# A mixture-of-experts stage in units of 128 rows instead of 256, written out with constant waits

## What is computed

```python
xn = layernorm(x)
x = x + gnn(xn, edges, weights) + linear_attention(xn)      # stages 1 and 2
h = layernorm(x)                                            # stage 3
gate_logits = h @ Wg + bg + bias                            # 8 experts
topk_vals, topk_idx = top_k(gate_logits, 2)
topk_w = softmax(topk_vals)
hid = relu(einsum('td,edh->teh', h, W1) + b1)               # 256 -> 512
y = einsum('teh,ehd->ted', hid, W2) + b2                    # 512 -> 256
x = x + sum over the two chosen experts of topk_w * y
```

## Time and profile before

| | us |
|---|---|
| median of 3 runs | 3915.12 |
| lowest and highest of them | 3912.13, 3915.24 |
| the profiled execution | 3911.73 |
| its span in the profile | 3910.0 |
| TensorE busy (share of the span) | 2910.5 (74%) |
| VectorE busy | 2598.6 (66%) |
| GpSimd busy | 2539.5 (65%) |
| mean granted TensorE clock | 0.898 of full speed |
| expert stage, first transposes to the last add's issue | 3056.66 to 3904.03 |

### The profile page before, as it was taken

How to read it: one execution, slowest core, us unless ns; L and a number is a source line. 1 busy time by engine, 2 the same in 40 slices (tenths; PEclk the granted TensorE clock), 3 DMA queues, 4 the chain that set the end, 5 groups by cost and what they waited for, 6 DMA issues and landing times. The chain is left out here.

```text
span 3910.0 us, 52671 instructions
## 1 busy us (share of the span) xinstructions
PE 2910.5 (74%) x16406; PEld 2397.2 (61%) x16407; DVE 2598.6 (66%) x6331; ACT 639.2 (16%) x1335; POOL 2539.5 (65%) x2431
## 2 busy tenths in 40 slices
PE   5957777476666666666776777777765799999998
PEld 5846666255555555555555555555532688888887
DVE  8899888165555555556888888888876444454444
ACT  8212222310000000000000000000023121222221
POOL 0048888577777777777777777777726478744444
PEclk9997777789898989888999898899887899999999
DMA  5857775533443433344444444444373365544443
GB/s 180 269 172 218 214 209 162 185 119 119 118 118 118 119 116 118 118 118 124 130 128 128 131 130 129 125 131 130 116 243 112 81 114 120 119 78 71 73 72 55
DMA packets 348241, 521.28 MB, mean 133 GB/s; under 512 B 54265, under 2 KB 267773, under 8 KB 348029
## 3 DMA queue, kind: packets, MB, share of 16 engines
q0 software_dynamic: 130944, 275.64, 28.0%
q1 hardware_dynamic: 166547, 187.72, 16.0%
q10 hardware_dynamic: 50537, 55.32, 4.5%
HBM read 378.21 MB, written 140.28 MB: 133 GB/s over the span
## 5 line engine op out<-in xcount | busy, mean ns | idle before, releaser
L721 POOL DMA_INDIRECT message<-h_table,records x1660 | 1597.2, 962 | 541.5 <-issue 527.0
L1213 PE MATMUL bank<-message,select 128*128 128x256 f32 x3320 | 894.7, 418 | 389.9 <-issue 344.8
L1780 DVE TENSOR_TENSOR acc<-acc,bank 128x256 f32 x1660 | 698.8, 421 | 552.1 <-PE bank L1213 383.8
L1213 PEld LDWEIGHTS bank<-message,select 128*128 128x128 f32 x3320 | 661.9, 207 | 577.0 <-issue 424.8
L682 POOL DMA_INDIRECT lists<-placed,dest_i x300 | 384.4, 1281 | 324.7 <-ACT placed L898 240.9
L765 POOL DMA_INDIRECT out<-acc,row_of x224 | 350.8, 1566 | 358.9 <-DVE acc L2189 236.5
L1773 DVE TENSOR_SCALAR select<-iota_n,records 128x128 f32<-128x128 f32 x1660 | 466.2, 361 | 14.6 <-ACT acc L939 12.7
L1461 PE MATMUL bank<-w,acc 128*128 x1792 | 407.6, 381 | 9.7 <-DVE acc L2173 9.5
L1448 PE MATMUL bank<-fx_t,acc 128*128 128x256 f32 x1792 | 406.6, 380 | 1.6 <-ACT fx_t L1034 1.6
L1448 PEld LDWEIGHTS bank<-fx_t,acc 128*128 128x128 f32 x1792 | 341.4, 191 | 48.7 <-issue 2.1
L1461 PEld LDWEIGHTS bank<-w,acc 128*128 128x128 f32 x1792 | 333.1, 191 | 52.4 <-issue 11.3
(11 more groups left out here) (305 smaller groups left out, 3664.2 us busy)
## 6 DMA issues: line engine op xcount, KB each, us to landing
rows<-block_dram SPq DMA_DIRECT2D x75, 514.5 KB
acc<-x_sorted SPq DMA_DIRECT2D x112, 260.0 KB, 2.9
message<-h_table,records POOLq DMA_INDIRECT x1660, 2.8
xt_in<-xt_dram SPq DMA_DIRECT2D x98, 256.0 KB, 3.0
x_sorted<-blank_rows ACTq DMA_DIRECT2D x42, 390.0 KB
lists<-zeros_list SPq DMA_DIRECT2D x8, 1664.0 KB, 15.2
read_back<-lists SPq DMA_DIRECT2D x13, 1024.0 KB, 6.6
x_sorted<-blank_rows SPq DMA_DIRECT2D x2, 6370.0 KB
```

The costliest lines, as they stand in the source:

```text
L721: pool.indirect_dma_start(out=message[:, k % SETS, j, :], out_offset=None, in_=h_table, in_offset=Offset(ap=records[:, k * SET + j, 0:1], ...
L1213: last = nc.tensor.matmul(ps, select[:, slot % 2, j, :], message[:, slot % SETS, j, :], start=True, stop=True)
L1780: added = V.tensor_tensor(to, to, ps, ALU.add)
```

## The change

- A unit is 128 rows. Half 0 has at most 91 units, half 1 at most 119: 210 in all, 26,880 rows where 28,672 were before.
- up multiplies 128 columns with each loaded W1 tile where it were 256; down has 4 matmuls of 256 columns where it were 8; x_transpose has 2 where it were 4. add_unit issues one indirect DMA and waits for all adds before it.
- fx has 8 slots of one group; hid_t, fy, fx_t and w1_now have 4 slots. finish(u) waits for the add of unit u-4.
- All units are written out on each engine, with constants in the waits in place of loops with registers. The expert is still read into registers, for 4 units at a time.
- route_half(1) is no generator any more and runs through before the first unit. GpSimd has two waits on it inside the sends of half 0 (before send 64 and send 72 of 84). The sends of half 1 begin ahead of the first add (12 of them) and are spread over the adds of the first 80 units.
- SyncE loads 8 units, then stores and loads half 1's table of experts, and then loads the others.
- The blank rows take one DMA for each stretch of x_sorted where it were two.

The core of the diff. For SyncE, TensorE and VectorE only the lines of the new text are shown; what they replace can be read in the kernel above. Left out are `x_transpose`, `copy_x`, `copy_w1` and `split_unit`, which change as the list says, and `route_half`, where only yield goes and the sizes 2 * P and the shift by 8 become P and 7:

```diff
-    UX = [(4 * n * P + EXPERTS * (2 * P - 1)) // (2 * P) for n in HALF_PAIRS]
+    UX = [(4 * n * P + EXPERTS * (P - 1)) // P for n in HALF_PAIRS]
     UXS = sum(UX)
-    GROUPS = UXS // 4
-    UNIT_RING = 4
-    ROUTED, AHEAD, SPREAD = 9, 6, 44
-    BESIDE = 3
-    assert (ROUTED + UNIT_RING + 3) % 4 == 0
-    assert PAIRS % TURN == 0 and max(UX) <= P and UXS % 4 == 0 and UX[0] % 4 == 1 and KH == 4
+    UNIT_RING, SLOTS_X = 8, 4
+    AHEAD, SPREAD = 12, 80
+    BESIDE, PICKED, ROUTED = 3, 64, 72
+    assert PAIRS % TURN == 0 and max(UX) <= P and KH == 4 and ROUTED < 4 * HALF_PAIRS[0]
...
+            eng.dma_start(x_sorted[half].rearrange("(t p) c -> p t c", p=P)[:, first:end, :],
+                          blank_rows[:, half, :].unsqueeze(1).to_broadcast([P, end - first, CR])).then_inc(s_blank, 16)
...
+            def load_unit(u):
+                half, unit = (0, u) if u < UX[0] else (1, u - UX[0])
+                if u >= UNIT_RING:
                     sp.wait_ge(s_fxt_psum, u - UNIT_RING + 1)
                     sp.wait_ge(s_marked, u - UNIT_RING + 1)
+                sp.dma_start(fx[:, u % UNIT_RING, :], x_units[half][unit]).then_inc(s_fx[u % UNIT_RING], 16)
             sp.wait_ge(s_sent[0], 4 * HALF_PAIRS[0] * 16)
             for u in range(UNIT_RING):
+                load_unit(u)
             sp.wait_ge(s_route_done, 2)
             store_experts(1)
             load_experts(1)
+            for u in range(UNIT_RING, UX[0]):
+                load_unit(u)
             sp.wait_ge(s_sent[1], 4 * HALF_PAIRS[1] * 16)
+            for u in range(UX[0], UXS):
+                load_unit(u)
...
-            def add_unit(u, slot, ring):
+            def add_unit(u):
                 pool.wait_ge(s_fy, u + 1)
-                if not (isinstance(u, int) and u == 0):
-                    pool.wait_ge(s_y_out, u * 32)
+                if u:
+                    pool.wait_ge(s_y_out, u * 16)
                 pass_gate()
-                for j in range(2):
-                    pool.indirect_dma_start(
-                        out=out, out_offset=Offset(ap=row_of[:, ring, j:j + 1], axis=0),
-                        in_=fy[:, slot, j, :], in_offset=None, compute_op=ALU.add).then_inc(s_y_out, 16)
+                pool.indirect_dma_start(
+                    out=out, out_offset=Offset(ap=row_of[:, u % UNIT_RING:u % UNIT_RING + 1], axis=0),
+                    in_=fy[:, u % SLOTS_X, :], in_offset=None, compute_op=ALU.add).then_inc(s_y_out, 16)
...
+                if i == PICKED:
+                    pool.wait_ge(s_route, 3)
+                    pass_gate()
+                if i == ROUTED:
+                    pool.wait_ge(s_route_done, 2)
+                    pool.wait_ge(s_fxn, PAIRS)
+                    pass_gate()
                 send(0, i)
             for turn in range(TURNS):
                 pool.wait_ge(s_kept[turn], 32 if turn == TURNS - 1 else 16)
+            pass_gate()
             sends, sent = 4 * HALF_PAIRS[1], 0
-            for u in range(UX[0]):
-                if u == ROUTED:
-                    pool.wait_ge(s_route_done, 2)
-                    pool.wait_ge(s_fxn, PAIRS)
-                    pass_gate()
-                while u >= ROUTED and sent < min(sends, AHEAD + sends * (u - ROUTED) // (SPREAD - ROUTED)):
+            for u in range(UXS):
+                while sent < min(sends, AHEAD + sends * u // SPREAD):
                     send(1, sent)
                     sent += 1
-                add_unit(u, u % 2, u % UNIT_RING)
-            assert sent == sends
-            for slot in range(1, 4):
-                add_unit(UX[0] - 1 + slot, slot % 2, slot)
-            with pool.Fori(UX[0] // 4 + 1, GROUPS) as m:
-                for slot in range(4):
-                    add_unit(m * 4 + slot, slot % 2, slot)
-            pool.wait_ge(s_y_out, 32 * UXS)
+                add_unit(u)
+            assert sent == sends and SPREAD < UX[0]
+            pool.wait_ge(s_y_out, 16 * UXS)
...
+            def up(u):
                 pe.wait_ge(s_w1_now, u + 1)
                 pe.wait_ge(s_fxt, u + 1)
+                if u >= SLOTS_X:
+                    pe.wait_ge(s_hid, u - SLOTS_X + 1)
                 for h in range(KH):
                     for k in range(KC):
+                        last = nc.tensor.matmul(bank[2 + u % SLOTS_X][:, h * P:(h + 1) * P],
+                                                w1_now[:, u % SLOTS_X, k * HID + h * P:k * HID + (h + 1) * P], fx_t[:, u % SLOTS_X, k, :],
                                                 start=(k == 0), stop=(k == KC - 1))
+                last.then_inc(s_hid_psum, 1)
+            def down(u, expert):
+                if u >= 2:
                     pe.wait_ge(s_y_read, u - 1)
+                pe.wait_ge(s_hid, u + 1)
+                for k in range(KH):
+                    last = nc.tensor.matmul(bank[6 + u % 2][:, 0:C], hid_t[:, u % SLOTS_X, k, :],
+                                            w2_flat[:, ds(expert + k * C, C)], start=(k == 0), stop=(k == KH - 1))
                 last.then_inc(s_fy_psum, 1)
+            expert_registers = [[pe.alloc_register(f"expert_{g}_{i}") for i in range(4)] for g in range(2)]
+            e = [None, None]
             pe.wait_ge(s_gate_read, TURNS)
+            pe.wait_ge(s_rank_out, 1)
+            x_transpose(0)
+            for u in range(UXS + 1):
+                if u % 4 == 0 and u < UXS:
+                    n = min(4, UXS - u)
+                    if u <= UX[0] < u + 4:
+                        pe.wait_ge(s_xtile_row[1], 16)
+                    e[u // 4 % 2] = load_offsets(pe, expert_registers[u // 4 % 2][0:n], xtile_row[:, 0, :], u, n,
+                                                 (EXPERTS - 1) * KC * HID)
+                if u < UXS:
+                    up(u)
+                if u + 1 < UXS:
+                    x_transpose(u + 1)
                 if u:
+                    down(u - 1, e[(u - 1) // 4 % 2][(u - 1) % 4])
...
+            def relu(u, expert):
+                dve.wait_ge(s_hid_psum, u + 1)
+                if u >= SLOTS_X:
+                    dve.wait_ge(s_fy_psum, u - SLOTS_X + 1)
                 for h in range(KH):
+                    last = V.tensor_scalar(hid_t[:, u % SLOTS_X, h, :], bank[2 + u % SLOTS_X][:, h * P:(h + 1) * P],
                                            table_flat[:, ds(expert + (C + h), 1)], 0.0, ALU.add, ALU.max)
+                last.then_inc(s_hid, 1)
+            def finish(u, expert):
+                if u >= SLOTS_X:
+                    dve.wait_ge(s_y_out, (u - SLOTS_X + 1) * 16)
+                dve.wait_ge(s_marked, u + 1)
                 dve.wait_ge(s_fy_psum, u + 1)
+                V.tensor_tensor(fy[:, u % SLOTS_X, :], bank[6 + u % 2][:, 0:C], table_flat[:, ds(expert, C)], ALU.add).then_inc(s_y_read, 1)
                 dve.wait_ge(s_y_read, u + 1)
+                V.tensor_scalar(fy[:, u % SLOTS_X, :], fy[:, u % SLOTS_X, :], share[:, u % UNIT_RING:u % UNIT_RING + 1], None,
+                                ALU.mult).then_inc(s_fy, 1)
+            expert_registers = [[dve.alloc_register(f"expert_{g}_{i}") for i in range(4)] for g in range(2)]
+            e = [None, None]
+            for u in range(UXS + 1):
+                if u % 4 == 0 and u < UXS:
+                    n = min(4, UXS - u)
+                    if u <= UX[0] < u + 4:
+                        dve.wait_ge(s_xtile_row[1], 16)
+                    e[u // 4 % 2] = load_offsets(dve, expert_registers[u // 4 % 2][0:n], xtile_row[:, 1, :], u, n, (EXPERTS - 1) * BT)
+                if u < UXS:
+                    split_unit(u, e[u // 4 % 2][u % 4])
+                    relu(u, e[u // 4 % 2][u % 4])
                 if u:
+                    finish(u - 1, e[(u - 1) // 4 % 2][(u - 1) % 4])
```

More of the change, by code:

```diff
@@ L133, in gps_layer @@
     xtile_dram = nc.dram_tensor("xtile_dram", (2, 2, P), I32, kind="Internal").ap()
-    x_sorted = [nc.dram_tensor(f"x_sorted{i}", (UX[i] * 2 * P, CR), F32, kind="Internal").ap() for i in range(2)]
+    x_sorted = [nc.dram_tensor(f"x_sorted{i}", (UX[i] * P, CR), F32, kind="Internal").ap() for i in range(2)]
     with ExitStack() as whole:
@@ L1051, in _ @@
             act.wait_ge(s_sent[0], 4 * HALF_PAIRS[0] * 16)
[L1052 to L1057, removed]
+            for u in range(UXS):
+                if u % 4 == 0:
+                    n = min(4, UXS - u)
+                    if u <= UX[0] < u + 4:
+                        act.wait_ge(s_xtile_row[1], 16)
+                    e = load_offsets(act, expert_registers[0:n], xtile_row[:, 0, :], u, n, (EXPERTS - 1) * KC * HID)
+                copy_w1(u, e[u % 4])
+                copy_x(u)
         @block.tensor
@@ L1450, in up @@
                                                 start=(k == 0), stop=(k == KC - 1))
[L1451 to L1456, removed]
+                last.then_inc(s_hid_psum, 1)
+            def down(u, expert):
+                if u >= 2:
                     pe.wait_ge(s_y_read, u - 1)
```

(43 more changed lines are left out.)

203 lines of the change are left out of this document (42 added, 161 removed).

## The result

The changed kernel takes 4075.39 us (median of 4 runs, 4071.69 to 4076.43) against 3914.72 us (median of 4 runs of the kernel before; the 3915.12 of the table above is that of 3): ratio 1.0412, 95% interval 1.04 to 1.0425. It is 4.1% slower, 1.4 us from the 4074 us predicted.

A forecast was written before the change was run, and what follows sets the result against it. TensorE paced the kernel before; GpSimd's chain of adds would take over: 3068 + 72 x 4.8 + 137 x 4.74 = 4063 us for the last add's start, 4074 us as median (4.1% slower), 8-in-10 range 4022 to 4130.

The forecast's parts named there:

- TensorE's unit, 3.73 us: Expert stage: up 1.78, transposes 0.22 and down 1.73 us per 128-row unit; 783 us for 210 units, 40 less than before.
- TensorE's busy share: Expert stage afterwards: TensorE has an idle gap in each unit and is busy near 79%.
- The cycle of an add: GpSimd's add_unit: each add waits out a whole landing plus 0.79 us, 4.74 us a unit, 4.8 with sends.
- The nominal 4.59: GpSimd's add cycle as 3.8 us landing plus 0.79 us; the mean of the plain stretch was 0.15 us above it.
- this chain takes over: Expert stage: GpSimd's one-by-one adds, 9.48 us for 256 rows against TensorE's 7.46, become the bound; chance 0.83.
- The start: Entry into the expert stage: first add at 3068, 7 us before 3075.02; the two new waits on routing cost nothing.
- The sends: GpSimd: 100 sends of half 1 among the adds of 72 units hide inside landings; 4.8 us a unit, 129 us if uncovered.
- the written-out loops: All engines: longer, unrolled programs without loops cost 0 to 5 us.
- the routing's place: Half 1's routing before the first unit: through by 3027, so both waits inside half 0's sends cost nothing.
- Blank rows and ScalarE's issues: 18 fewer issues of blank rows, in a stage where ScalarE is busy 104 of 400 us: nothing, at best some 10 us.
- The rival of the clock: TensorE, idle a fifth of each unit, gets clock 0.75, so a unit costs 4.97 us: 4145 us in all; chance 0.10.

The follow-up runs named there:

- experiment 7: Changed kernel, but from unit 8 on SyncE loads only the last 4 of 260 columns of each row, 16 bytes for 1040: 4042.03 us, ratio 1.0328.
- experiment 1: Changed kernel, but odd units add to a second tensor with its own count, so an add waits for the one before the last: 3858.42 us, ratio 0.986.
- experiment 6: Changed kernel with add_unit writing its rows to out without accumulating: 3854.96 us, ratio 0.9853.
- 10: Changed kernel, but an add may go out while the one before is under way if both units have the same expert; output whole: 3854.85 us, ratio 0.9856.
- experiment 2: Kernel before, units of 256 rows and loops, but a unit's second add also waits for the first to land: 4186.93 us, ratio 1.0703.
- experiment 8: Changed kernel with all 112 sends of half 1 ahead of the first add: 4188.48 us, ratio 1.0706.
- 3: Kernel before with its hardware loops over units written out, constants in the waits, units still 256 rows: 3912.35 us, ratio 0.9997.
- 4: Kernel before, but VectorE runs half 1's routing to its end before the first unit: 3914.14 us, ratio 1.0.
- experiment 5: Changed kernel with 2 of the 4 matmuls of each unit in down: 4062.15 us, ratio 1.0388.
- experiment 9: Changed kernel without the semaphore increment (pass_gate) between the wait and the add in add_unit: 4067.41 us, ratio 1.0394.

## Why the prediction was right

- **TensorE's unit, 3.73 us.** Measured 3.73. Line 1266 of another stage was a good neighbour: the record of 128 columns behind a fresh load costs 1.79 / 16 = 0.112 us. So the weight loads don't show, though each one's record is 0.197 us long (line 1428, mean). The Trainium skill (TensorE: Matmul & The Clock Gate, Part 3, The mechanism) says that a load overlaps running matmuls only when the row groups differ; for this pattern that is not so. The same section also has loads pulled ahead into a background weight buffer, which would fit; no run here shows the buffer.
- **TensorE's busy share.** Forecast near 79%, measured 85% (511 of 600 us). The 127 units of that window hold 4.0 us of busy time each and not 3.73; its clock of 0.97 would account for about 0.1 of the 0.3 us, the rest stays open. It cost nothing, since TensorE was not the bound.
- **The cycle of an add.** 4.74 predicted for plain units, 4.73 measured; 4.8 for units with sends, 4.83 measured. It came from a stretch of the kernel before in which GpSimd was catching up. The nominal 4.59 would have given some 30 us less; experiment 7 shows that the difference is the loads running beside the adds: without them a cycle takes 4.58.
- **That this chain takes over.** Shown from both sides: taken away in the changed kernel (experiments 1, 6, 10), put into the kernel before (2).
- **The start.** First add forecast at 3068, measured 3067.87; the last one forecast at 4063, measured 4063.94. Half 1's routing was through before 3023, where 3027 was allowed, so neither new wait held the sends. That the start agrees to 0.1 us is luck: in the experiments whose edits lie behind the entry into the stage, the first transposes start anywhere from 3053.45 to 3063.22 and the first add from 3064.68 to 3074.62 (experiment 8 aside). The 1.4 us of the whole are luck to that extent; the cycle, which carries 995 us of the sum, is not.
- **The sends.** The 0.06 us over the plain cycle that the prediction gave each of the 72 units with sends are 4 us; in the profile these units cost 0.10 us more than the rest (7 us), and experiment 8 saves 15 us over all adds. They lie inside the landings nearly, not wholly.
- **Costed at nothing, or next to it, and found so:** the written-out loops (3), the routing's place (4). Blank rows and ScalarE's issues were not tried by themselves; the sorting stage's end did not move (the last send of half 0 stands at 3051.25, for 3051.30).
- **The rival of the clock** did not come. I had feared 0.75 to 0.90 with TensorE idle for a fifth; it was busy 85% and the clock 0.97. Even with 72% busy (experiment 5) it was 0.93, and with 86% (experiment 7, the same window) 1.00. The clock thus isn't settled by the busy share alone (the earlier trace rows has 0.75 and 0.90 at 70 to 71%), and which feature of those stages keeps it lower stays open.

The same accounts say what the change was worth in its parts: smaller units bring some 55 us (1.4%, experiment 1), and the one-by-one adds take 217 us back. Of the 55, 40 are 1,792 fewer rows (823 to 783 us on TensorE, an estimate). An earlier start is not among them: in experiment 1 the first add starts at 3074.62, for 3075.02 before. What the rest is stays open.

## What to carry to other kernels

Before a unit of work is halved, ask which waits it pays for once per unit: each link in a chain of dependent DMAs costs issue to landing plus wake-up (here 3.8 and 0.79 us), and a busy share doesn't show it. Look in the old trace for a stretch in which the suspected engine is catching up, since there its own pace stands bare, contention included. If order is needed only between some neighbours, make the wait depend on that rather than on the count of all that went before.

## What the runs showed of the hardware

- An accumulating indirect DMA of 128 rows of 1024 bytes lands 3.8 to 3.9 us after its issue (medians of the kernel before and of experiments 5 and 7), a plain one of the same size after 2.4 us (experiment 6); GpSimd's record is 1.55 to 1.59 us for the one and 0.97 for the other.
- Adding keeps the DMA engines about twice as busy as writing. From 3400 to 3800 us they are busy 44% of the time in experiment 1 and 23% in experiment 6, while both move 72 GB/s by the profile.
- From a landing to the start of the add that waited for it are 0.75 us (experiment 9), and 0.79 us with an increment of a semaphore between (experiment 2).
- A load of 130 KB that runs beside each add lengthened the cycle by some 0.15 us (4.73 for 4.58 us over 137 units, experiment 7).
- f32 matmul records of 128 columns, each behind a fresh weight load whose own record is 0.197 us, start 0.112 us apart at full clock (the changed kernel, `up`).
